# Loading whole 32 KB rows of adj, 4 MB at a time, in a graph attention kernel

## The reference, cut to what matters

```python
h  = relu(layernorm(x))                    # 8192 x 64
Wh = h @ W
e  = leaky_relu((Wh @ a1)[:, None] + (Wh @ a2)[None, :], 0.2)
scores = where(adj > 0, e, -9e15)
out = x + elu(softmax(scores, axis=1) @ Wh)
```

## Time and profile before

| | |
|---|---|
| median of 3 runs | 693.45 us (692.99 to 693.48) |
| the profiled execution | 694.66 us, of which the span of the profile is 692.8 us |
| busy in the span | PE 632.5, ACT 631.4, DVE 621.0, POOL 53.4 us |
| moved by DMA | 275.15 MB, 397 GB/s over the span |

### The profile page before, as it was taken

One profiled execution on the slowest core, in us unless ns is written; L12 is line 12 of the kernel. 1 busy time (PEld: TensorE's weight loads), 2 busy tenths in 40 slices (PEclk: granted clock), 3 DMA queues, 4 the chain that ended last, 5 costly groups with the idle time before them and its releaser, 6 DMA issues.

```text
span 692.8 us, 23845 instructions
## 1 busy us (share of the span) xinstructions
PE 632.5 (91%) x10422; PEld 621.6 (90%) x10422; DVE 621.0 (90%) x625; ACT 631.4 (91%) x366; POOL 53.4 (8%) x51
## 2 busy tenths in 40 slices
PE   4867999999998989989898998989898998989895
PEld 4747999999998989989898998989898998989895
DVE  5898979999999899898989899898989989898983
ACT  4797999999999989989898998989899898989881
POOL 5000001011000101010010101001010100001010
PEclk9987999999999999999999999999999999999998
DMA  9876899999999999999999999999999999999960
GB/s 323 360 292 260 347 374 386 422 429 425 428 425 430 427 427 429 424 430 425 429 424 429 428 427 425 427 429 425 429 427 426 428 426 429 424 429 427 427 293 19
DMA packets 24840, 275.15 MB, mean 397 GB/s; under 512 B 3088, under 2 KB 7440, under 8 KB 8432
## 3 DMA queue, kind: packets, MB, share of 16 engines
q1 hardware_dynamic: 22864, 270.67, 93.3%
q0 software_dynamic: 1488, 4.07, 1.5%
q10 hardware_dynamic: 464, 0.07, 0.1%
HBM read 272.70 MB, written 2.10 MB: 397 GB/s over the span
## 4 chain that ended last, share of the span: by engine, by line
DMA 32%; DVE 29%; ACT 22%; issue 11%; PE 5%; DVEq 1%; ACTq 1%; SPq 0%
DMA adj_ring<-in_adj 31%; DVE code L651 18%; ACT work L513 16%; DVE work L664 4%; ACT work L521 4%; DVE code L658 1%; PE psum L876 1%; PE psum L896 1%; PE psum L894 1%; PE psum L827 1%; DMA Wx<-in_L_gnn_W 1%; PE psum L817 1%; DVE last_steps L682 1%; DVE last_steps L686 1%; ACT trow L496 1%
## 5 line engine op out<-in xcount | busy, mean ns | idle before, releaser
L896 PE MATMUL psum<-V,work 128*128 128x130 f16 x4096 | 495.3, 221 | 0.0
L894 PE MATMUL psum<-V,work 128*128 128x130 f16 x4096 | 495.0, 220 | 0.0
L513 ACT ACTIVATE work<-trow,Wh 128x4096 int8<-128x4096 f32 x128 | 476.8, 3725 | 0.0
L894 PEld LDWEIGHTS psum<-V,work 128*128 128x128 fp8e4 x4096 | 403.1, 98 | 0.0
L896 PEld LDWEIGHTS psum<-V,work 128*128 128x128 fp8e4 x4096 | 398.7, 97 | 0.0
L651 DVE TENSOR_SCALAR code<-adj_ring 128x4096 uint8<-128x4096 int32 x128 | 293.3, 2292 | 32.7 <-DMA adj_ring<-in_adj 32.7
L876 PE MATMUL psum<-identb,code 128*128 128x128 bf16 x2048 | 137.0, 220 | 41.7 <-DVE code L658 41.6
L658 DVE SCALAR_TENSOR_TENSOR code<-work,code 128x1024 int32<-128x1024 int32 x128 | 156.8, 1225 | 7.9 <-ACT work L513 4.0
L876 PEld LDWEIGHTS psum<-identb,code 128*128 128x128 bf16 x2048 | 119.8, 98 | 48.0 <-DVE code L658 30.8
L521 ACT COPY work<-psum 128x1024 int32<-128x1024 int32 x128 | 129.8, 1014 | 35.9 <-PE psum L876 35.9
L664 DVE TENSOR_SCALAR work<-work 128x1024 int32<-128x1024 int32 x128 | 87.9, 686 | 1.7 <-ACT work L521 1.7
(11 more groups left out here) (76 smaller groups left out, 151.3 us busy)
## 6 DMA issues: line engine op xcount, KB each, us to landing
adj_ring<-in_adj SPq DMA_DIRECT2D x128, 2048.0 KB, 16.9
work<-in_x SPq DMA_DIRECT2D x4, 512.0 KB, 6.0
last_steps<-in_x POOLq DMA_DIRECT2D x16, 128.0 KB, 6.6
out_y<-last_steps POOLq DMA_DIRECT2D x15, 128.0 KB, 7.8
out_y<-last_steps SPq DMA_DIRECT2D x1, 128.0 KB, 1.9
W<-in_L_gnn_W ACTq DMA_DIRECT2D x2, 16.0 KB, 5.4
Wx<-in_L_gnn_W ACTq DMA_DIRECT2D x2, 16.0 KB, 5.6
a_sb<-in_L_gnn_a ACTq DMA_DIRECT2D x1, 0.5 KB, 3.9
```

The source lines that it names most:

```text
L513: nc.scalar.activation(sign[:, k % 2].bitcast(I8), trow[:, h * UW:(h + 1) * UW], ACT.Sign, bias=(Wh[:, B, 0:1] if isinstance(B, int) else ...
L894: nc.tensor.matmul(sums_of[:, 0:FP], up8[:, j // 2, j % 2], V[:, jb, 0:FP], start=h == 0 and j == 0, stop=False, skip_group_check=True)
L896: last = nc.tensor.matmul(sums_of[:, FP:2 * FP], down8[:, j // 2, j % 2], V[:, jb, FP:2 * FP], start=False, stop=h == 1 and j == HB - 1, s ...
```

## The change

The first body is as before. From the second on (`by_halves(i)` is false), SP loads a whole block, 128 rows of 32 KB or 4 MB, in one transfer into one of two places of the same ring (the SBUF space is the same), each with a semaphore of its own (`s_rows`). Units 2b and 2b+1 of a body are now the two halves of block b. The wait ahead of load b is for `edges` of unit 2b-3, counted in its body: the second half of the block two before. The order of operations on DVE, ACT and PE is unchanged; what a unit number stands for is changed, and so are the counts that `copy_lows` waits for (pair 0 is complete after unit 3, was after unit 5).

```diff
-        def block_and_half(k):
-            return k % KE, k // KE
+        def by_halves(i):
+            return isinstance(i, int) and i == 0
+        def block_and_half(i, k):
+            return (k % KE, k // KE) if by_halves(i) else (k // 2, k % 2)
...
-                def load_when_free(i, k, c):
-                    sp.wait_ge(s_edge, (i * BU + k) * UT + c - RT + 1)
-                    load(i, k, c)
+                def load_rows(i, b):
+                    sp.wait_ge(s_edge, i * BU + 2 * b + 2 - RT)
+                    t = b % 2
+                    sp.dma_start(adj_ring[:, 2 * t:2 * t + 2, :].rearrange("p t w -> p (t w)"),
+                                 adj_v[b // 2, b % 2][bass.ds(i, 1)].rearrange("o p j -> p (o j)")).then_inc(s_rows[t], 16)
...
                 with sp.Fori(1, NI) as i:
-                    for k in range(BU):
-                        for c in range(UT):
-                            load_when_free(i, k, c)
+                    for b in range(KE):
+                        load_rows(i, b)
...
-                    act.wait_ge(s_mult, RC + i * BU + KE + 2 * o + 2)
+                    act.wait_ge(s_mult, RC + i * BU + (KE + 2 * o + 2 if by_halves(i) else 4 * o + 4))
...
                     dve.wait_ge(s_T, i * BU + k + 1)
...
+                    if by_halves(i):
+                        dve.wait_ge(s_adj[k % KE], k // KE * 16 + 16)
+                    else:
+                        dve.wait_ge(s_rows[k // 2 % 2], (i - 1) * 32 + (k // 4 + 1) * 16)
+                    nc.vector.tensor_scalar(code[:, k % RM, :], adj_ring[:, k % RT, :], 0.0, float(EDGE), ALU.is_gt, ALU.mult)\
+                        .then_inc(s_edge, 1)
```

More of the change, by code:

```diff
@@ L43, in build_gat @@
     TW = UW
-    UT = UW // TW
     RT = 4
@@ L56, in build_gat @@
     TR = 8
-    assert JB % (2 * NR) == 0 and JB % KE == 0 and 2 * F == P and HP % 2 == 0 and RT == UT * KE
+    assert JB % (2 * NR) == 0 and JB % KE == 0 and 2 * F == P and HP % 2 == 0 and RT == KE
     ctx = ExitStack()
@@ L179, in build_gat @@
         s_adj = [sem(f"adj_loaded_{t}") for t in range(RT)]
+        s_rows = [sem(f"rows_of_adj_loaded_{t}") for t in range(2)]
         s_edge = sem("edge_codes_of_a_tile_written")
@@ L387, in _, with load_half @@
                                      xs[:, r * PR:(r + 1) * PR]).then_inc(s_x[r], 16)
[L389 to L397, removed]
-                def load_when_free(i, k, c):
-                    sp.wait_ge(s_edge, (i * BU + k) * UT + c - RT + 1)
-                    load(i, k, c)
-                for k in range(BU):
-                    for c in range(UT):
[L405 to L408, removed]
+                def load_half(k):
+                    b, h = block_and_half(0, k)
+                    sp.dma_start(adj_ring[:, b, :], adj_v[b // 2, b % 2][0, :, h * UW:(h + 1) * UW]).then_inc(s_adj[b], 16)
+                def load_rows(i, b):
[3 more added lines that the diff above has]
+                                 adj_v[b // 2, b % 2][bass.ds(i, 1)].rearrange("o p j -> p (o j)")).then_inc(s_rows[t], 16)
+                for k in range(BU):
+                    if k >= KE:
+                        sp.wait_ge(s_edge, k - RT + 1)
+                    load_half(k)
                 with sp.Fori(1, NI) as i:
-                    for k in range(BU):
-                        for c in range(UT):
-                            load_when_free(i, k, c)
+                    for b in range(KE):
+                        load_rows(i, b)
                 sp.wait_ge(s_res, NI)
@@ L508, in step @@
                 def step(i, k):
-                    b, h = block_and_half(k % BU)
-                    B = (i + k // BU) * KE + b
+                    if k >= BU:
+                        return step(i + 1, k - BU)
+                    b, h = block_and_half(i, k)
+                    B = i * KE + b
                     nc.scalar.activation(sign[:, k % 2].bitcast(I8), trow[:, h * UW:(h + 1) * UW], ACT.Sign,
@@ L645, in edges @@
                 def edges(i, k):
+                    if k >= BU:
+                        return edges(i + 1, k - BU)
                     dve.wait_ge(s_T, i * BU + k + 1)
[L648 to L652, removed]
+                    if by_halves(i):
[4 more added lines that the diff above has]
+                        .then_inc(s_edge, 1)
                 def codes(i, k):
-                    dve.wait_ge(s_edge, (i * BU + k + 1) * UT)
+                    dve.wait_ge(s_edge, i * BU + k + 1)
                     dve.wait_ge(s_sign, i * BU + k + 1)
@@ L879, in multiply_unit @@
                 def multiply_unit(i, k, first=False):
-                    b, h = block_and_half(k)
+                    b, h = block_and_half(i, k)
                     o = b // 2
```

## The result

The changed kernel takes 731.16 us (median of 4 runs, 728.79 to 732.43), against 693.47 for the kernel before (4 runs on the same chips): a ratio of 1.0537, 95% interval 1.0505 to 1.0570, slower. The forecast was 724.5 us, range 708 to 742. The profiled execution took 730.2 us, its span 728.4.

The account below looks back on a forecast made before the run. The DMA engines were taken to bound the kernel. Late refills over the bodies (+24.7 us), start (+2.3) and end (+4.1) summed to +31.1, moving the median from 693.45 to 724.5 us, range 708 to 742.

Parts of the forecast that it names:

- What bounds the kernel, and compute: Steady bodies: DMA engines never idle at 39.90 us a body; compute needs under 38 us and stays under the loads.
- Packets: Adj loads: 32 KB rows halve the packets at 9.4 ns each; 4 MB takes 9.75 us, gaining 4.5 us in all.
- The refill of block 3: Block 1's place is freed 9.24 us after landing, block 3 lands at 21.27 against 19.50: 1.77 us lost each body.
- The three loads called hidden: Refills of blocks 2, next 0 and next 1 cost nothing, save 0.3 us a body, bounds 0 and 2.
- Start and end: First bodies: adj lands 2.3 us later; last block: both halves land together, so the end comes 4.1 us later.
- The sum: Whole run: +24.7 us for the bodies, +2.3 and +4.1 make +31.1; median from 693.45 to 724.5 us.
- dearer refills: Rival, chance 0.15: each load issued under 4 us ahead pays up to 2 us a body, not 0.3; 748 us.

Follow-up runs that it names:

- the order of the units alone: Changed kernel's unit order, but adj in 2 MB loads into four places, each freed by its own `edges`, as before the change: 693.84 us, ratio 1.0002.
- both edges together: Changed kernel with both `edges` of a block directly one behind the other on DVE from the second body on, sums behind them: 696.92 us, ratio 1.0062.
- the two-load kernel: Changed kernel with each block as two 2 MB loads of 16 KB rows, issued together and both waited for by `edges`: 738.9 us, ratio 1.065.
- The reduction ahead of `edges(3)`: Changed kernel plus an unused 1.22 us DVE reduction between the two `edges` of block 1, from the second body on: 747.26 us, ratio 1.0770.
- the sums behind `edges`: Changed kernel with `take_sums` and `divide` placed behind `edges` instead of ahead of it on DVE: 737.12 us, ratio 1.0616.
- the run without small transfers: Changed kernel without output stores in bodies 3 to 13, and x loaded for 16 partitions of 128 there: about 738 us, ratio 1.0641.
- the reduction ahead of `edges(5)`: Changed kernel plus the same unused DVE reduction between the two `edges` of block 2: about 757 us, ratio 1.0918.

## Why the prediction was right, and where it was not

- **What bounds the kernel, and compute**: right. The busy times in a body are unchanged, and the order of the units alone costs nothing (1.0002).
- **Packets**: the right mechanism. Large packets nearly halved, and 4 MB take 9.7 us back to back (9.75 forecast). Where loads run evenly (200 to 600 us), a packet of 32 KB took 1.222 us on average with both edges together, and two of 16 KB took 1.232 in the kernel before: 10 ns saved, against 9.4 forecast, or 4.8 us over the 480 packets of an engine, against 4.5. Between the two-load kernel and the changed one it was 7.7 us, more than the price of the packets alone.
- **The refill of block 3**: right to 0.2 us. 6.66 us between the two `edges` (6.65), 11.9 to 12.1 us from issue to landing (12.03), 21.1 us from block 1 to block 3 (21.27). The reduction ahead of `edges(3)` entered nearly one to one.
- **The three loads called hidden**: only block 2's was (9.7 us after the one before). Blocks 0 and 1 came 10.5 and 10.2 us after theirs, where the bytes of x and output would explain 0.3 each beyond 9.75. The forecast kept 0.3 us a body for this, with 2 as its bound; it was about 0.5. That this came so near is luck, since 0.3 was a choice and not worked out, and the same cost is about 1 us on each load of the kernel with the sums behind `edges`. Over 13 bodies, from block 0 of body 2 to block 0 of body 15, it was 41.90 us a body:

```profile
L403 SPq DMA_DIRECT2D adj_ring<-in_adj x1: 333/333/333, 111.2 to 111.2; - x1
...
DMA to landing us min/median/max: 15.8/15.8/15.8
...
L403 SPq DMA_DIRECT2D adj_ring<-in_adj x1: 333/333/333, 657.4 to 657.4; - x1
...
DMA to landing us min/median/max: 14.4/14.4/14.4
```

  (671.8 - 127.0) / 13 = 41.9, against 41.69. Of the 33.4 us by which the changed kernel's span exceeds that of the kernel with both edges together, 11 are packets that took longer (above). That leaves 22 for idle engines, near the 24.8 us (1.77 x 14) at which the dry spells were forecast.
- **Start and end**: too small. The load of body 2's block 0 landed at 127.0, where it was 122.8 before: +4.2, not +2.3. The last landing, at 691.0 + 13.2 = 704.2, is 24.2 us before the end of the span, not 19.5: +4.7, forecast +4.1.
- **The sum**: 37.7 us between the medians, 35.6 between the spans, 31.1 forecast. Of the 4.5 between the spans and the forecast, start and end make 2.5. The other 2.0 lie between the landing of body 2's block 0 and the last one: 577.2 us, against 550.5 before, +26.7 where +24.7 was forecast. The 2.1 by which the medians differ more than the spans come from the choice of the profiled executions.
- **The step that failed** is the criterion behind "hidden": that a load costs nothing extra once its issue plus 12.03 us is earlier than the landing ahead plus 9.75. In the changed kernel it nearly held. As a rule it is wrong, as the sums behind `edges` showed: by it, that kernel had no dry spell left and should have taken 697 to 706 us; it took 737. The rival "dearer refills" named this effect, at a chance of 0.15, and had 748 us for it in the changed kernel. Its evidence was set aside because code was being loaded at the time; it should have weighed more.

The traces say where the packets are stretched. A load runs on 16 engines and has landed when the last of them is done. From 200 to 600 us the first engine is done 0.6 us ahead of the last in the changed kernel, 2.2 us with the sums behind `edges`, and 1.6 us with both edges together. So the loads of the kernel with the sums behind, issued 4.0 us ahead of the landing on average, are only 1.8 us ahead of the first engine; with both edges together it is 4.9 and 3.3. The middle packet of adj takes 1.21 to 1.22 us in all three, but 15% of them take over 1.35 us with the sums behind, 6% in the changed kernel and 0.6% with both edges together. Compare the loads of two kernels that are issued equally far, 3.9 to 4.6 us, ahead of the landing. With the sums behind there are 20; they are 1.9 us ahead of the first engine, and their packets take 0.6 us longer in all on each engine. With both edges together there are 10; they are 2.6 us ahead of it, and their packets take 0.1 us longer. It fits that the changed kernel's block 2 lost nothing: it is issued 2.7 us ahead of the landing, but its engines are so close together that this is 2.0 us ahead of the first.

This is read from traces; no run was made to test it. It would put the criterion at the first engine that is done, not at the landing. What stays open is why the engines drift apart, and why the run without small transfers and the one with the reduction ahead of `edges(5)` lost more than any theory here gives.

## What to carry to other kernels

What one wait covers should not be larger than what one step consumes: in the same SBUF, doubling the transfer and its place turned a line of some three loads of 2 MB into one load of 4 MB, and cost 5%. With places still freed 4 MB at a time but each half waited for alone, it cost 0.6%. The rate of large rows (430 GB/s instead of 427) was reached only where the place was emptied at once. Work out the time from landing to the next issue for each place, with all that stands between its consumers in program order, and ask for a good margin over the transfer ahead, 4 to 5.6 us here with the 16 engines within 1.6 us of each other, not merely for a positive one.

## What the runs showed of the hardware

- A DMA line can be busy 0.99 of the time and still lose some 7% of its rate (399 GB/s against 427 to 430). Here some 15% of the packets were stretched, from 1.21 us to over 1.35, in a line of at most two loads. The busy share alone doesn't show a DMA line at its peak; the rate beside it does.
- From issue to landing, 4 MB took 11.9 to 12.1 us with the line dry, and 9.7 us apart when in line: a restart costs 2.3 us. After the issue at 398.3 us the first packets started 1.0 to 1.5 us later and took 1.6 to 2.0 us instead of 1.21. The Trainium skill ("DMA: Bandwidth & Descriptors", the anatomy of one DMA) gives a fixed part of 2.0 us for a transfer that GpSimd issues, which makes an estimate of 11.6 for 4 MB; the trace, where SP issues, is 0.3 to 0.5 us above it.
- Leaving out 11 stores and most of 11 loads of x did not make the kernel faster (about 738 us against 731).
